# Two 3x3 convolutions as 64x32 array tiles over four-row slabs, row sums on GpSimd, one buffer for two normalised samples

## What is computed

```python
x = x + _L0_conv_ref(_gn(x), ...)   # 3x3 convolution, reflect padding; its weights are a mix of
                                    # three experts, by a softmax over the sample's channel means
x = x + _L1_conv_ref(_gn(x), ...)   # 3x3 depthwise convolution of abs(.), zero padding
x = x + _L2_conv_ref(_gn(x), 8)     # 17x17 box mean
x = x + _L3_conv_ref(_gn(x), ...)   # sum of the 8 neighbours, then a pixelwise network of
                                    # five layers (64 wide, four of them with elu)
```

## Time and profile before

| | us |
|---|---|
| median of 3 runs (950.04 to 955.53) | 951.59 |
| the profiled execution | 948.61 |
| its span, first to last instruction | 946.8 |

### The profile page before, as it was taken

The page is one execution under the profiler, slowest core; times in us unless marked ns, Lnnn a source line. Parts: engine busy times, 40 slices in busy tenths (PEclk is TensorE's granted clock), DMA queues, the critical chain, the costliest instruction groups (busy, mean ns, idle before and its releaser), DMA issues.

```text
span 946.8 us, 9275 instructions
## 1 busy us (share of the span) xinstructions
PE 821.2 (87%) x2377; PEld 396.0 (42%) x2377; DVE 741.6 (78%) x1264; ACT 597.4 (63%) x1105; POOL 226.9 (24%) x296
## 2 busy tenths in 40 slices
PE   1658786888999899998999899989999898979993
PEld 1423433343444445453545344444545353524331
DVE  2644674857989788988989798988888689877994
ACT  0020212566777768686777768686869477978883
POOL 2030234111522115121512142121511122131000
PEclk9988887989999999999999999999999999999997
DMA  5425432514120320205020311123020202001201
GB/s 98 78 38 90 85 50 61 95 27 68 14 54 25 59 41 17 61 17 81 11 66 11 65 22 43 34 48 50 17 62 19 46 18 61 17 17 33 63 17 44
DMA packets 68751, 43.18 MB, mean 46 GB/s; under 512 B 5602, under 2 KB 62306, under 8 KB 68722
## 3 DMA queue, kind: packets, MB, share of 16 engines
q1 hardware_dynamic: 66976, 42.57, 23.6%
q10 hardware_dynamic: 1746, 0.27, 0.3%
HBM read 9.67 MB, written 8.39 MB: 19 GB/s over the span
## 4 chain that ended last, share of the span: by engine, by line
PE 40%; DVE 25%; ACT 11%; DMA 10%; issue 5%; SPq 5%; POOL 2%; DVEq 0%; ACTq 0%; POOLq 0%
PE pz L696 21%; PE pc L640 7%; DVE g L891 6%; DMA xs<-in_x_dram 5%; ACT u L582 4%; DMA halo<-y 4%; DVE bn L812 3%; SPq L392 3%; ACT u L574 3%; PE pc L665 3%; DVE box_sum L928 3%; PE pc L655 3%; DVE u L887 3%; DVE box_sum L943 2%; PE pc L668 2%
## 5 line engine op out<-in xcount | busy, mean ns | idle before, releaser
L574 ACT ACTIVATE u<-pz 128x512 f32<-128x512 f32 x472 | 277.9, 595 | 180.8 <-PE pz L696 141.2
L696 PE MATMUL pz<-g,wT 128*128 128x512 f32 x768 | 363.3, 613 | 8.8 <-DVE g L891 8.2
L891 DVE SCALAR_TENSOR_TENSOR g<-u,pz 128x512 f32<-128x512 f32 x476 | 308.3, 682 | 72.8 <-ACT u L582 69.4
L582 ACT ACTIVATE u<-u 128x512 f32<-128x512 f32 x472 | 286.5, 635 | 1.3
L696 PEld LDWEIGHTS pz<-g,wT 128*128 128x128 f32 x768 | 145.7, 195 | 199.2 <-issue 127.1
L812 DVE BATCH_NORM_STATS2 bn<-xs 128x6 f32 (+1 forms) x128 | 87.1, 688 | 29.9 <-DMA xs<-in_x_dram 20.0
L655 PE MATMUL pc<-y,t 128*128 128x512 f32 x192 | 93.0, 622 | 8.0 <-DVE t L362 8.0
L665 PE MATMUL pc<-y,t 128*128 128x512 f32 x192 | 93.5, 625 | 2.4 <-ACT y L548 2.4
L692 PE MATMUL pz<-stack,w1T 128*128 128x512 f32 x256 | 80.4, 443 | 14.3 <-DMA stack<-near_rest 11.2
L459 POOL TENSOR_TENSOR st<-nv,con 128x1 f32<-128x1 f32 x32 | 17.9, 559 | 262.2 <-DVE nv L832 262.2
L471 POOL TENSOR_TENSOR near_part<-box_sum,near_part 128x512 fp32r<-128x512 f32 x32 | 40.9, 1288 | 148.5 <-ACT near_part L563 148.5
(11 more groups left out here) (108 smaller groups left out, 730.4 us busy)
## 6 DMA issues: line engine op xcount, KB each, us to landing
halo<-y SPq DMA_DIRECT2D x96, 120.0 KB, 3.3
xs<-in_x_dram SPq DMA_DIRECT2D x8, 1024.0 KB
stack<-near_rest SPq DMA_DIRECT2D x64, 128.0 KB, 2.3
out_dram<-xs SPq DMA_DIRECT2D x8, 1024.0 KB
stack<-stack SPq DMA_DIRECT2D x32, 128.0 KB, 2.2
halo<-y SPq DMA_DIRECT2D x48, 8.0 KB, 2.7
g<-in_con_late_dram SPq DMA_DIRECT2D x1, 712.0 KB, 10.2
con<-in_con_early_dram SPq DMA_DIRECT2D x1, 272.5 KB, 15.5
```

What stands on the lines that cost most here:

```text
L574: act.activation(u[:, m, :], pz[:, m, :], ACT.Relu, scale=-1.0, bias=0.0).then_inc(relu_done, 1)
L582: act.activation(u[:, m, :], u[:, m, :], ACT.Exp, scale=-1.0).then_inc(exp_done, 1)
L696: pe.matmul(pz[:, m, :], wT[:, l - 1, :], g[:, m, :], start=True, stop=True).then_inc(z_mm, 1)
L891: dve.scalar_tensor_tensor(out=elus(j, q, l)[:, m, :], in0=u[:, m, :], scalar=-1.0, in1=pz[:, m, :], op0=ALU.add, op1=ALU.max).then_inc(g_ ...
```

## The change

- Slabs. A strip of two output rows (2 rows x 16 channels = 32 outputs) needs four input rows (4 x 16 = 64 partitions), which are a slab; each of the four strips m of a block of eight rows takes its slab from one half of a window tensor. `win0` and `win1` are two tensors of 128 x 16 x 130 each, together four slabs, filled from `y0` and `y1` by SP. Which half of the partitions holds a slab alternates between the first and second half of k, so that the two chunks n and n + 2, done together, read different halves.
- `conv_pair` replaces `conv_chunk` for k < 2: 24 matmuls of 64 rows x 32 columns (three kw, four strips m, two chunks h), no halo matmul. Two pairs make a sample; PSUM bank h holds chunk n + 2h. The pairs stand at layers 0 and 2 in phase 0, and at 1 and 3 in phase 2 (`PAIR_AT`); DVE evacuates in the order 0, 2, 1, 3 (`EVAC_AT`).
- SP issues 12 DMAs for `win1` (5 after the first half of `y1`, 5 and 2 after the second) in place of 6 halo DMAs, and 14 for `win0` in place of 12.
- `near_sums` moves from DVE to POOL, between the four `lower_near`.
- `y3` is `y1`: `normal1` waits for the last evacuation of the neighbours of two samples before, `normal3` waits for `win1`.
- `spread` builds `t0` (now 128 x 3 x 32) with 5 operations instead of 12; `mix` loses the three operations on `whmix`; the matmul with `neg_group` goes, and POOL multiplies by -1 instead.

```diff
+        PAIR_AT = ((0, 2), (1, 3))
+        EVAC_AT = (((0,), (2,), (1,), (3,)), ((), (0,), (2,), (1, 3)), ((0,), (1,), (2,), (3,)), ((0,), (1,), (2,), (3,)))
+        def around(y, win, h, last):
+            a, b = h * WIN, WIN - h * WIN
+            lo, hi = h * K // 2, (h + 1) * K // 2
+            first, end = max(lo, 1), min(hi, K - 1)
+            if last:
+                return [(win[1][b + 3 * C:b + 4 * C, lo:end], y[0:C, lo + 1:end + 1])]
+            return [(win[0][b:b + WIN, lo:hi], y[C:5 * C, lo:hi]),
+                    (win[1][a:a + WIN, lo:hi], y[3 * C:7 * C, lo:hi]),
+                    (win[0][a + C:a + WIN, lo:hi], y[0:3 * C, lo:hi]),
+                    (win[0][a:a + C, first:hi], y[7 * C:P, first - 1:hi - 1]),
+                    (win[1][b:b + 3 * C, lo:hi], y[5 * C:P, lo:hi])]
...
-            def halos1(i):
-                sp.wait_ge(y1_written, 2 * i + 2)
-                for kw in range(3):
...
-                        sp.dma_start(dst, rows).then_inc(halo1_in, 16)
+            def windows1(i):
+                for h in range(2):
+                    sp.wait_ge(y1_written, 2 * i + h + 1)
+                    for dst, rows in around(y1, win1, h, False):
+                        sp.dma_start(dst, rows).then_inc(win1_in, 16)
+                for h in range(2):
+                    for dst, rows in around(y1, win1, h, True):
+                        sp.dma_start(dst, rows).then_inc(win1_in, 16)
...
                 if late:
-                    for c in range(Q):
-                        lower_near(t, c)
+                    near_sums(t, 0)
+                    near_sums(t, 1)
+                    lower_near(t, 0)
+                    near_sums(t, 2)
+                    lower_near(t, 1)
+                    near_sums(t, 3)
+                    lower_near(t, 2)
+                    lower_near(t, 3)
...
+            def conv_pair(i, k, n, last_conv):
+                if n:
+                    pe.wait_ge(conv_evac[k], Q * i + 2)
+                elif last_conv:
+                    pe.wait_ge(conv_evac[last_conv[0]], Q * last_conv[1] + Q)
+                if n == 0 and k == 0:
+                    pe.wait_ge(spread_step, SPREAD * i + SPREAD)
+                    pe.wait_ge(win0_in, WIN0 * i + WIN0)
...
+                    pe.wait_ge(win1_in, WIN1 * i + WIN1)
+                pe.nop(nofuse=True)
+                mat, win = (t1, win1) if k else (t0, win0)
+                for kw in range(3):
+                    for m in range(4):
+                        for h in range(2):
+                            rows = slice((m + h) % 2 * WIN, (m + h) % 2 * WIN + WIN)
+                            last = pe.matmul(pc[2 * C * m:2 * C * m + 2 * C, h, :], mat[rows, kw, :],
+                                             blocks(win[m // 2], n + 2 * h)[rows, :, kw:kw + W], start=kw == 0, stop=kw == 2)
+                last.then_inc(conv_mm[k], 1)
...
             def normal3(i):
                 dve.wait_ge(norm_step[3], i * NORM + NORM)
+                if not (isinstance(i, int) and i == B - 1):
+                    dve.wait_ge(win1_in, WIN1 * (i + 2))
```

More of the change, by code:

```diff
@@ L103, in build @@
         y2 = sb("y2", [P, K * PITCH + BOX])
-        y3 = sb("y3", [P, K, W + 2])
-        halo0 = sb("halo0", [HALO, K, W])
-        halo1 = sb("halo1", [HALO, K, W])
+        y3 = y1
+        win0 = [sb(f"win0_{n}", [P, K, W + 2]) for n in range(2)]
+        win1 = [sb(f"win1_{n}", [P, K, W + 2]) for n in range(2)]
         box_sum = sb("box_sum", [P, 2, KB * PITCH])
@@ L162, in build @@
         bn = [sb(f"bn{k}", [P, Q, 6]) for k in range(4)]
[L164 to L167, removed]
+        stat = sb("stat", [P, 4, 9])
+        ms = [stat[:, k, 0:2] for k in range(4)]
+        gs = [stat[:, k, 2:5] for k in range(4)]
+        nv = [stat[:, k, 5:7] for k in range(4)]
+        st = [stat[:, k, 7:9] for k in range(4)]
         pooled = sb("pooled", [C, 1])
@@ L546, in normal1 @@
                 act.wait_ge(norm_step[1], i * NORM + NORM)
+                if not (isinstance(i, int) and i < 2):
+                    act.wait_ge(conv_evac[3], Q * (i - 1))
                 rows = slice(half * K // 2, (half + 1) * K // 2)
@@ L721, in one @@
                             logits(t + 2)
-                        if conv:
+                        if conv and conv[0] > 1:
                             conv_chunk(conv[1], conv[0], l, before(t, p, early, late))
+                        elif conv and l in PAIR_AT[conv[0]]:
+                            conv_pair(conv[1], conv[0], PAIR_AT[conv[0]].index(l), before(t, p, early, late))
             def spread_channels():
@@ L731, in spread_channels @@
                 pe.matmul(pc[:, 0, 510:511], const("spread", C), bias_in[:, :], start=True, stop=True)
[L732 to L738 removed]
+                pe.matmul(pc[:, 0, 440:440 + EXPERTS], const("ones", 1), fcb_in[:, :], start=True, stop=True).then_inc(setup_pe, 1)
             pe.wait_ge(s_early, 16)
@@ L976, in one @@
                                 mix(t + 2)
-                        if p == 2 and late:
-                            if l == 1:
-                                normal3(t)
-                                near_sums(t, 0)
-                                near_sums(t, 1)
-                            if l == 2:
-                                near_sums(t, 2)
-                            if l == 3:
-                                near_sums(t, 3)
+                        if p == 2 and late and l == 1:
+                            normal3(t)
                         if p == 3 and early:
```

193 lines of the change are left out of this document (74 added, 119 removed).

## The result

The changed kernel takes 913.87 us (median of 4 runs, 912.17 to 915.07), where the kernel before took 952.92 beside it: ratio 0.959, 95% interval 0.9553 to 0.9626. It is 39 us faster; forecast were 61.

A forecast was written before the change was run, and what follows sets the result against it. PE was taken to lead, busy 97.47 of 102.7 us a round, with DVE close at 89.03. -54.6 + 2 - 8 = -61 us on the profiled 948.61 gave 888, and 891 us as median; range 868 to 932.

The forecast's parts named there:

- case A: Whole kernel: the terms hold as summed, 891 us, own range 868 (also given as 870) to 908; chance 0.60.
- B: Convolution pairs on PE: two row halves don't run at once, a pair takes 5.2 us, time 929; chance 0.17.
- C: Near sums on POOL: row sums cost more and POOL is the bound; 920 at 1.8 us an add; chance 0.08.
- D: Window DMAs in SP's one queue land late, each us after 434 costing one in six rounds; 915 at 438; chance 0.07.
- The pair: Convolution on PE: 24 tiles, eight at once, take 2.6 us, so a sample takes 5.2 us and not 13.8.
- E: Convolution pairs on PE: tiles hardly overlap and the kernel gets slower, 1038 with two at once, some 1330 one by one; chance 0.08.
- Phase 2: Second convolution's phase: 22 to 24 us where it took 33.10, with PE's wait for DMAs below 2 us, one layer later.
- POOL's adds: Near sums on POOL: 1.05 to 1.3 us an add, POOL busy 35 us a round, ACT waiting 4 us together.
- Phases 2 and 3 together: Rounds 1 to 6: each gains 9.1 us, -54.6 us in all.
- Phase 0: First convolution's phase: no change (from -1.2 to +2), since DVE has 26.29 us to do there whatever PE does.
- Rounds -1 and 0: Start, without the network: shorter convolutions and `spread`, less near sums on POOL, give -8 us, between -3 and -15.
- Round 7: No convolution beside the near sums: the POOL chain, 12 us where DVE took 7, adds about 2 us.

The follow-up runs named there:

- experiment 4: Changed kernel with both chunks of a pair reading the same half of the rows, so at most four tiles run at once: 961.9 us, ratio 1.0106.
- experiment 1: Changed kernel with DVE evacuating each convolution 0 chunk in phase 0 straight behind the joins, ahead of scan and statistics: 895.24 us, ratio 0.9418.
- experiment 7: Changed kernel with convolution 0 chunks evacuated straight behind the joins and sample loads issued ahead of the window DMAs: 880.96 us, ratio 0.9239.
- experiment 10: Kernel before with one part of the change alone, the near sums moved from DVE to POOL: 946.18 us, ratio 0.9903.
- experiment 3: Changed kernel with the near sums back on DVE, at the places they had in the kernel before: 943.68 us, ratio 0.9924.

## Why the prediction was right and wrong

The direction was right and the time was inside the range. Part of that is luck: case A's own range ended at 908, and 913.87 is covered only by the times of rivals B to D, of which B and C did not happen and D did only at the start. (A's lower end is given as 868 and as 870 in one sentence of the prediction; its own terms give 870. Nothing hangs on it.) The likeliest case was 23 us too fast: its mechanism held in phases 2 and 3, and two terms had the wrong sign or size.

- *The pair, 2.6 us*: right. 2.81 us with its tail, and 5.41 where only four tiles can run. Rivals B and E are out. By the Trainium skill's rule (TensorEngine Tiling (Array Packing), Restrictions and Gotchas) different row tiles can't use one PSUM bank at the same time, which would have meant a pair about as long as in experiment 4. The trace doesn't agree: 2.81 us and not 5.41, with tiles of both row halves writing each of the two banks, in different strips of 32 partitions. The measurement decides.
- *Phase 2*: right. The pair started 9.9 us into the phase (9 to 11 forecast), PE waited 1.32 us for windows (under 2), the phase took 23.1 to 23.3 (22 to 24). So rival D is out for the rounds.
- *POOL's adds*: 1.04 and 1.19 us by the means of their groups (1.05 to 1.3). Rival C is out. POOL was busy for 32.95 us of a round, near the 35. ACT's waits for the sums came to 2.6 us in round 3 (0.46 and 2.11), and not to 4.

```profile
L478 POOL TENSOR_TENSOR box_sum<-box_sum,y 128x512 f32<-128x512 f32 x32 | 38.0, 1186 | 2.5
L476 POOL TENSOR_TENSOR box_sum<-y 128x512 f32<-128x512 f32 x32 | 33.3, 1041 | 32.6 <-DVE y L951 31.4
```

- *Phases 2 and 3 together, -54.6*: -51.0. Phase 3's second layer stood at 451.23, 30.7 us after the start of phase 2, where 29.7 was forecast, behind a wait of 2.52 us for the merge of the statistics (449.53), of which 0.84 is the small DVE step that lasted until POOL was done. In round 3 the layer behind it took 3.59 us; in round 4, behind a wait of 2.53, it took 5.19 at a granted clock of 0.93 (1.00 in round 3). That is the other 1.8 us, in every second round.
- *Phase 0, "can't become shorter than that, whatever PE does"*: this failed twice. The bound was no bound: it took DVE's busy time in the old order as fixed, with scans that were long beside POOL's work, and it took PE's phase for DVE's. PE's phase was 24.9 us in the changed kernel, while DVE's took 28.07; with experiment 1 they were 23.3 and 24.70. And the price of the late second pair, 0 to +2 on phase 0, was looked for in the wrong phase: phase 0 fell by 2.6, and phase 1 grew by 4.6 to 5.8. What was missing is the chain behind the second pair (evacuation, statistics, merge, group sums, which PE's own program waits for), and the clock of PE after waits of 2 to 3 us. These phases lost 10.5 us in the changed kernel; with the order mended they fell by 28, of which phases 2 and 3 gave back 7.5 and the median shows 18. The prediction named "a phase 0 that grows with the late second pair" and a lower clock as what could make it wrong; both came, the first in phase 1.
- *Rounds -1 and 0, -8*: this failed, +8.7. The step that failed first is the wait of `normal3` for `win1`, priced at nothing because the pair "needs the same DMAs anyway". In the rounds that holds. In round 0 `normal3` was held for 8.55 us by the late windows, and the near sums, `spread` and the network come behind it. From `normal3` to the split of the network's first chunk on POOL it is then 18.5 us and not 20.0 (156.41 - 137.91, and 148.00 - 128.02), near the 2 us less that were forecast for `spread` and the sums together. No run gives `y3` a buffer of its own, so that this wait is the cause is read from the trace and not shown by an experiment.
- *The same term, what the pairs and windows should have given*: the convolutions were priced at full clock, and they ran at 0.62 to 0.68, since PE has little else there: 4.1 to 5.4 us for a pair. Filling PE gave 3 us of the start in the profiled executions. The first 2.6 us of work beside the halo DMAs were rightly taken off, but the windows' issue was counted at "one or two" more: for conv 1 it is 12 against 6, 9 us of issue with nothing beside it. And the loads, "don't shorten", were pushed back and pushed the windows back: with the loads early (experiment 7) the last window of conv 1 landed 3.94 us after its issue and not 10.95.
- *Round 7, +2*: -1.8. The sums on POOL are the cause: alone they bring it from 82.8 to 81.1 us (experiment 10), and with them back on DVE (experiment 3) it takes 84.5. That DVE is then free for the network's joins is the likely reason, and isn't shown by itself.
- *Granted clock 1.0 in phases 0, 1 and 3*: it is 0.93 in all three in round 4, and 0.93, 0.87 and 1.00 in round 3; in phase 2 it is 1.00 in both.

## What to carry to other kernels

When an operation becomes so short that it is done in two bursts, its results are used as a group: look at what stands in the consumer's program ahead of the first result that the second burst needs, and follow the delay past the end of the phase, to the statistics and sums that hang on it. Moving work off the leading engine pays in full only where the next bound in the same phase is moved too; here each of two parts alone gave 1%, and both 4%. A DMA count that doubles on one queue is paid twice, in issue time where nothing hides it and in the place that later loads get in the queue. A buffer that two stages share adds a wait; price it where DMAs are latest, at the start, and not only in the repeated round. And busy time isn't fixed work: an operation can be long because another engine runs beside it.

## What the runs showed of the hardware

- Tiles of 64 rows by 32 columns from both halves of the rows, writing the same PSUM banks in different strips, ran eight at once: 24 float32 matmuls of 512 columns in 2.81 us, and in 5.41 us where the eight matmuls of one kw shared four tiles.
- DVE operations lasted longer beside POOL's: a scan of 128x580 took 1.36 us with POOL idle and 2.28 with a POOL subtraction of 1.19 us beside it, and a 128x1 step of 0.22 us took 1.06, ending with POOL's operation.
- A wait of PE can be paid again in what follows. After 2.38 us idle a pair took 4.33 us; with the same stretch filled by idle matmuls, 2.81. After waits of 0.2 to 1.3 us pairs of the rounds took 2.81. It isn't the wait alone: in phase 3, behind 2.5 us of it, a layer took 3.59 us in one round and 5.19 in the next, as in this row (PE's timeline, round 4):

```profile
545.28 0.38 PE L646 MATMUL psm<-stat,con 128*128 128x2 f32 x2 [2.53 <-DVE stat L836]
545.52 1.74 PE L659 MATMUL pc<-near_part,near_mat 128*128 128x512 f32 x6
547.07 5.19 PE L719 MATMUL pz<-g,wT 128*128 128x512 f32 x8
```

- At the start, where the granted clock fell to 0.62, a single matmul record of the pair lasted 1057 ns at the median, 587 at the least.
- SP's issue of a window DMA took 0.53 to 1.27 us at the start, 0.60 at the median, and its landing 4.4 to 4.6 us at the median over the run, but 10.95 us where the windows followed on a load of 1 MB (in round 0), and 3.94 in the same place with the loads early.
